# A decoder layer on one core: a third table of expert tiles, row scatters over more tiles, and another order at the end

## The reference

```python
x = _layernorm(x + _L0_attn_ref(x, ...))          # 16 heads of 16, over 1024 tokens
x = _layernorm(x + _L0_xattn_ref(x, ctx_1024, ...))  # one head, 77 context rows
x = _layernorm(x + _L0_ffn_ref(x, ...))           # 8 experts, 2 for each token
```

```python
gate = jax.nn.softmax(xf @ gate_w + gate_b)
topv, topi = jax.lax.top_k(gate, K)               # K = 2
topv = topv / topv.sum(-1, keepdims=True)
...
h = jax.nn.relu(xf @ w1e + b1e)                   # 256 -> 1024
y = h @ w2e + b2e                                 # 1024 -> 256
return (acc + y * ce[:, None], None)
```

## Time and profile before

| | us |
|---|---|
| median of 3 runs | 1412.01 |
| lowest and highest | 1411.73, 1417.89 |
| the profiled execution's own time | 1415.77 |
| span in its trace | 1413.8 |
| PE busy in the span | 1363.8 |
| DVE busy | 1063.5 |
| ACT busy | 858.8 |
| POOL busy | 592.2 |
| mean granted TensorE clock | 0.991 |

### The profile page before, as it was taken

One profiled execution on the slowest core, in us unless ns is written; L12 is line 12 of the kernel. 1 busy time (PEld: TensorE's weight loads), 2 busy tenths in 40 slices (PEclk: granted clock), 3 DMA queues, 4 the chain that ended last, 5 costly groups with the idle time before them and its releaser, 6 DMA issues.

```text
span 1413.8 us, 49461 instructions
## 1 busy us (share of the span) xinstructions
PE 1363.8 (96%) x18332; PEld 981.6 (69%) x18332; DVE 1063.5 (75%) x1989; ACT 858.8 (61%) x1903; POOL 592.2 (42%) x1058
## 2 busy tenths in 40 slices
PE   9999999999999999999999899989988999999995
PEld 5445454577777765456554458988877999999995
DVE  6888888888888888889999865756655566666564
ACT  4688888888887877778887784653222333333331
POOL 3221212222323224542223523566775556555555
PEclk9999999999999999999999999999999999999998
DMA  6236545544444323422423343333433333333332
GB/s 207 79 93 184 170 146 168 140 125 124 113 121 140 90 68 90 124 80 66 149 75 88 92 164 98 88 104 90 138 116 93 91 95 96 96 94 95 93 96 65
DMA packets 149816, 157.04 MB, mean 111 GB/s; under 512 B 68971, under 2 KB 121514, under 8 KB 148554
## 3 DMA queue, kind: packets, MB, share of 16 engines
q1 hardware_dynamic: 134922, 114.25, 29.8%
q0 software_dynamic: 14080, 38.32, 8.1%
q10 hardware_dynamic: 576, 1.31, 0.3%
HBM read 90.74 MB, written 63.04 MB: 109 GB/s over the span
## 4 chain that ended last, share of the span: by engine, by line
PE 77%; DVE 7%; issue 6%; POOL 5%; DMA 1%; ACT 1%; SPq 1%; another core or an unknown queue 1%; DVEq 1%; POOLq 0%; ACTq 0%
PE pa L1048 15%; PE pb L1048 14%; PE po L1220 14%; PE pa L1294 13%; PE pb L1308 11%; PE px L1048 8%; DVE neg L1582 3%; PE pb L1041 1%; POOL y_parts L995 1%; POOL out L989 1%; POOL x_by_expert L901 1%; PE px L1041 1%; DMA space<-y_parts,y_tags 1%; ACT w_sb L1414 1%
## 5 line engine op out<-in xcount | busy, mean ns | idle before, releaser
L1582 DVE TENSOR_REDUCE neg<-pa 128x1 f32<-128x1024 f32 x512 | 611.6, 1213 | 66.6 <-PE pa L1048 53.0
L1414 ACT ACTIVATE w_sb<-pb 128x512 f32<-128x512 f32 x996 | 589.2, 599 | 112.7 <-PE pb L1048 74.1
L1048 PE MATMUL pb<-w_sb 99*32 99x512 bf16 x3984 | 417.2, 381 | 5.8 <-ACT w_sb L1414 3.2
L1512 ACT ACTIVATE space<-pa,b1T_sb 128x128 f32<-128x128 f32 x568 | 154.6, 383 | 318.3 <-PE pa L1294 159.6
L1048 PE MATMUL pa<-w_sb 96*32 96x512 bf16 (+1 forms) x4208 | 335.3, 379 | 6.0 <-DVE neg L1582 5.5
L1220 PE MATMUL po<-w_sb,space 128*32 128x256 f32 x4000 | 315.6, 379 | 0.4 <-issue 0.3
L1294 PE MATMUL pa<-xgT,attn_t 128*128 128x128 f32 x2272 | 271.7, 278 | 14.8 <-DVE xgT L1869 11.8
L1294 PEld LDWEIGHTS pa<-xgT,attn_t 128*128 128x128 f32 x2272 | 268.1, 194 | 23.5 <-DVE xgT L1869 15.5
L1308 PE MATMUL pb<-w_sb,space 128*128 x1136 | 263.0, 382 | 0.4 <-issue 0.4
L1308 PEld LDWEIGHTS pb<-w_sb,space 128*128 128x128 f32 x1136 | 211.2, 192 | 27.0 <-issue 1.1
L1048 PEld LDWEIGHTS pa<-w_sb 96*32 96x32 bf16 (+1 forms) x4208 | 127.9, 97 | 109.3 <-DVE neg L1582 34.0
(11 more groups left out here) (251 smaller groups left out, 1230.7 us busy)
## 6 DMA issues: line engine op xcount, KB each, us to landing
y_parts<-attn_t SPq DMA_DIRECT2D x13, 896.0 KB, 4.9
xg<-x_by_expert SPq DMA_DIRECT2D x71, 130.0 KB
w_sb<-w SPq DMA_DIRECT2D x17, 512.0 KB, 4.6
attention_out<-space SPq DMA_DIRECT2D x64, 128.0 KB
w_sb<-w SPq DMA_DIRECT2D x7, 1024.0 KB
q_parts<-w_sb SPq DMA_DIRECT2D x48, 128.0 KB, 3.1
w_sb<-q_parts SPq DMA_DIRECT2D x64, 96.0 KB, 2.3
w_sb<-k_parts SPq DMA_DIRECT2D x64, 96.0 KB, 2.4
```

What stands on the lines that cost most here:

```text
L1048: mm = pe.matmul(out[at:end], lhsT[:, at:end], rhs, start=start, stop=stop, tile_position=(0, at))
L1414: act.activation(ex_of(n)[:, half * HALF:(half + 1) * HALF], score_bank(n, half), ACT.Exp, scale=SCALE).then_inc(e_done, 1)
L1512: ins = act.activation(hT[tile % 2][:, f, :], pH[tile % 2][:, f, :], ACT.Relu, bias=g.b1_sb[:, bass.ds(e * FT + f, 1)])
L1582: dve.tensor_reduce(neg[i % 2][:, t:t + 1], pa[n % 2][:, :], AX.X, ALU.max, negate=True).then_inc(max_done, 1)
```

## The change

It has five parts.

1. A table in the middle, `TABLE_M`, is made from batches 0 to 2 and covers tiles 25 to 40 (`MIDDLE` = 41). `later_tiles` replaces `late_tiles` and makes both later tables. The new one takes four stages, at the ends of token tiles 6 to 9 on VectorE, in rooms of their own (`hot`, `both`). The last table covers 30 tiles instead of 46.
2. SyncE's wait ahead of tile 25 asks for the middle table and batch 2's second rows; the wait for batch 3, the last table and the padding moves to tile 38, ahead of tile 41.
3. The row scatters go one to a tile from tile 7, two in tiles 12, 15, 18, 21, 24 and 27 (`TWO_ROWS` + 2), the last in tile 32.
4. GpSimd's order in the last two tiles: `scatter(69)` goes ahead of `scatter_out(68)`, and `gather(70)` ahead of `spread_3(69)`; `scatter_out(70)` counts on a semaphore of its own and no longer waits for `scatter_out(69)` to land.
5. VectorE reads the last tile's expert number from `table` at the start of tile 70 instead of just ahead of its `raw`.

```diff
-    EARLY = 3 * TB + 1
+    EARLY, MIDDLE = 3 * TB + 1, 5 * TB + 1
...
-    ROWS_AT = range(5, 21)
+    TWO_ROWS = (10, 13, 16, 19, 22, 25)
+
+    def rows_at(since):
+
+        first = sum(2 if n in TWO_ROWS else 1 for n in range(5, since))
+        return [row for row in range(first, first + (2 if since in TWO_ROWS else 1)) if since >= 5 and row < 4 * TB]
...
+        TABLE_M = TABLE_2 + ["left_1", "left_2", "left_3", "early"]
...
                         if tile + 3 == EARLY:
+                            sp.wait_ge(table_1, len(TABLE) + len(TABLE_M))
+                            sp.wait_ge(second_rows[B - 2], 16 * TB)
+                        if tile + 3 == MIDDLE:
                             sp.wait_ge(table_2, len(TABLE_2))
-                            for b in range(2, B):
-                                sp.wait_ge(second_rows[b], 16 * TB)
+                            sp.wait_ge(second_rows[B - 1], 16 * TB)
                             sp.wait_ge(pads_in, 16 * NE)
...
                     pool.wait_ge(c_normed, tile + 1)
-                    if tile:
+                    if 0 < tile < FFN_TILES - 1:
                         pool.wait_ge(out_rows, 16 * tile)
                     settle(pool, settled_pool)
                     pool.indirect_dma_start(g.out, bass.IndirectOffsetOnAxis(y_tag[tile % TAGS][:, 3:4], 0),
-                                            x3[tile % YS], None, bounds_check=Y_ROWS - 1).then_inc(out_rows, 16)
+                                            x3[tile % YS], None, bounds_check=Y_ROWS - 1
+                                            ).then_inc(out_rows if tile < FFN_TILES - 1 else last_out, 16)
...
-                    rows = [2 * (since - ROWS_AT[0]) + i for i in range(2)] if since in ROWS_AT else []
+                    rows = rows_at(since)
...
                     if LAST_TOKENS + 1 < tile < FFN_TILES - 1:
                         scatter_out(tile - 2)
+                    if tile == FFN_TILES - 1:
+                        scatter_out(tile - 2)
+                        gather(tile)
                     if tile:
                         spread_3(tile - 1)
...
-                    gather(tile)
+                    if tile < FFN_TILES - 1:
+                        gather(tile)
                     for row in rows[len(ahead):]:
                         scatter_row(row)
-                    if with_tokens(tile) or tile == FFN_TILES - 2:
+                    if with_tokens(tile):
...
+                def later_tiles(stage, first, last):
+                    n = last - first
+                    done, names = (len(TABLE), TABLE_M) if last < FFN_TILES else (0, TABLE_2)
+                    made = table_1 if last < FFN_TILES else table_2
+
+                    def after(name):
+                        dve.wait_ge(made, done + names.index(name) + 1)
...
+                        up_to = 0 if last < FFN_TILES else P - 1
+                        dve.tensor_scalar(full_i[:, :], g.run[:, :], float(up_to), None, ALU.add).then_inc(made, 1)
...
+                    if stage == 3:
+                        after("row_0")
+                        dve.tensor_tensor(left[:, :], tiles[:, :], cum[:, :], ALU.subtract).then_inc(made, 1)
+                        after("left_1")
+                        dve.tensor_scalar(left[:, :], left[:, :], float(n), 0.0, ALU.add, ALU.max).then_inc(made, 1)
+                        after("left_2")
+                        dve.tensor_tensor(left[:, :], left[:, :], tiles[:, :], ALU.min).then_inc(made, 1)
+                        after("left_3")
+                        dve.tensor_tensor(early[:, :], early[:, :], left[:, :], ALU.add).then_inc(made, 1)
...
-                def raw(tile):
-                    e = number(dve, tile, 1)
+                def raw(tile, e=None):
+                    e = number(dve, tile, 1) if e is None else e
...
+                    if SHIFT + 4 <= tile < SHIFT + 8:
+                        later_tiles(tile - SHIFT - 4, EARLY, MIDDLE)
...
-                    if since >= 4:
-                        late_tiles(since - 4)
+                    if 4 <= since < 7:
+                        later_tiles(since - 4, MIDDLE, FFN_TILES)
...
                 for tile in range(FFN_TILES):
+                    if tile == FFN_TILES - 1:
+                        last_e = number(dve, tile, 1)
...
-                result(FFN_TILES - 1)
+                result(FFN_TILES - 1, last_e)
```

More of the change, by code:

```diff
@@ L333, in stream @@
         top_f = sb("top_f", [P, TB, 2])
-        hot = [sb(f"hot{i}", [P, TB, NE]) for i in range(2)]
+        hot_room = sb("hot", [P, 2 * TB * NE])
+        hot = [hot_room[:, i * TB * NE:(i + 1) * TB * NE].rearrange("p (t e) -> p t e", e=NE) for i in range(2)]
         both = sb("both", [P, TB, NE])
@@ L1801, in early_tiles @@
                         dve.tensor_tensor(early[:, :], early[:, :], tiles[:, :], ALU.min).then_inc(table_1, 1)
-                def late_tiles(stage):
-                    n = FFN_TILES - EARLY
-                    slots = g.step_c[:, g.col["tiles"]][:, 0:n]
-                    past = late_room[:, 0:n * NE].rearrange("p (t e) -> p t e", e=NE)
-                    expert, before_e = (late_room[:, n * (NE + i):n * (NE + i + 1)] for i in range(2))
+                def later_tiles(stage, first, last):
[4 more added lines that the diff above has]
+                        dve.wait_ge(made, done + names.index(name) + 1)
+                    slots = g.step_c[:, g.col["tiles"]][:, 0:n]
+                    if last < FFN_TILES:
+                        past = hot_room[:, 0:n * NE].rearrange("p (t e) -> p t e", e=NE)
+                        expert, before_e = (both_room[:, n * i:n * (i + 1)] for i in range(2))
+                    else:
+                        past = late_room[:, 0:n * NE].rearrange("p (t e) -> p t e", e=NE)
+                        expert, before_e = (late_room[:, n * (NE + i):n * (NE + i + 1)] for i in range(2))
@@ L1814, in late_tiles @@
-                        dve.wait_ge(table_2, tabled_2("shift"))
-                        dve.tensor_copy(tiles[:, :], full_i[:, :]).then_inc(table_2, 1)
-                        dve.wait_ge(table_2, tabled_2("tiles"))
-                        dve.tensor_tensor(tiles[:, :], tiles[:, :], early[:, :], ALU.subtract).then_inc(table_2, 1)
-                        dve.wait_ge(table_2, tabled_2("late"))
-                        settle(dve, g.settled)
-                        dve.tensor_tensor_scan(cum[:, :], g.ones[:, 0:NE], tiles[:, :], 0.0, ALU.mult, ALU.add).then_inc(table_2, 1)
@@ new lines, in later_tiles @@
+                        after("shift")
+                        dve.tensor_copy(tiles[:, :], full_i[:, :]).then_inc(made, 1)
+                        after("tiles")
+                        dve.tensor_tensor(tiles[:, :], tiles[:, :], early[:, :], ALU.subtract).then_inc(made, 1)
+                        after("late")
+                        settle(dve, g.settled)
+                        dve.tensor_tensor_scan(cum[:, :], g.ones[:, 0:NE], tiles[:, :], 0.0, ALU.mult, ALU.add).then_inc(made, 1)
+                        dve.tensor_tensor(step[:, 0:NE - 1], early[:, 1:NE], early[:, 0:NE - 1], ALU.subtract).then_inc(made, 1)
@@ new lines, in later_tiles @@
+                        dve.tensor_scalar(step[:, NE - 1:NE], early[:, NE - 1:NE], -1.0, None, ALU.mult).then_inc(made, 1)
+                        after("step_last")
+                        dve.tensor_tensor(step[:, :], tiles[:, :], step[:, :], ALU.subtract).then_inc(made, 1)
+                    if stage == 1:
+                        dve.tensor_tensor(past, wide(slots, False, n), wide(cum[:, :], True, n), ALU.is_ge).then_inc(made, 1)
+                        after("past")
+                        dve.tensor_reduce(expert, past, AX.X, ALU.add).then_inc(made, 1)
+                        after("expert")
+                        dve.tensor_tensor(past, past, wide(step[:, :], True, n), ALU.mult).then_inc(made, 1)
+                        after("weighted")
+                        dve.tensor_reduce(before_e, past, AX.X, ALU.add).then_inc(made, 1)
@@ new lines, in later_tiles @@
+                    if stage == 2:
+                        after("before")
+                        dve.tensor_tensor(before_e, slots, before_e, ALU.subtract).then_inc(made, 1)
+                        after("row")
+                        dve.tensor_scalar(before_e, before_e, early[:, 0:1], None, ALU.add).then_inc(made, 1)
+                        after("row_0")
+                        dve.tensor_scalar(before_e, before_e, float(P), None, ALU.mult).then_inc(made, 1)
+                        after("rows_128")
+                        dve.scalar_tensor_tensor(g.table[:, 0, first:last], expert, float(ROWS_E), before_e, ALU.mult,
+                                                 ALU.add).then_inc(made, 1)
+                        dve.tensor_scalar(g.table[:, 1, first:last], expert, float(NE - 1), None, ALU.min).then_inc(made, 1)
@@ L1994, in raw, with result @@
```

(4 more changed lines are left out.)

39 lines of the change are left out of this document (11 added, 28 removed).

## The result

The changed kernel takes **1395.19 us** (median of 4 runs, 1393.45 to 1398.06); the kernel before, with one more run beside the three above, takes 1413.77. The ratio is 0.9867, with a 95% interval of 0.9837 to 0.9897: faster by 1.3%. I had forecast 1392.7 from 1412.01, a ratio of 0.9863. Its span is 17.7 us shorter than that of before; tiles 12 to 24 alone are 19.1 us shorter.

A forecast was written before the change was run, and what follows sets the result against it. TensorE was taken as the bound, losing 20.9 us in tiles 12 to 24, with GpSimd the engine to budget. Terms -20.9 + 3.7 + 1.0 - 5.3 + 2.7 - 0.5 = -19.3 us gave 1392.7 from median 1412.01; range 1386 to 1404.

The forecast's parts named there:

- The wait moves: SyncE's wait, tile 22 to 38: passed without stopping, removing 8.3 us of idle time and slow clock at tile 24.
- Row scatters over tiles 7 to 32, padding, last table: Tiles 12 to 32: the 12.6 us lost over tiles 12 to 23 replaced by losses of 3.7 and 1.0.
- The 1.0 for padding and last table: Tiles 13 to 16: VectorE's padding and last-table work still loses 1.0 us, bounds 0 and 3.
- The 3.7 for GpSimd: Tiles 12 to 32: GpSimd's 151.4 us of work exceeds 147.7, all 3.7 taken as loss; bounds 0 and 14.
- GpSimd's budget: Plain tiles: 5.31 us of own work plus 1.3 per row scatter, 6.61 with one and 7.91 with two.
- Token tiles: Tiles 7 to 10: one row scatter instead of two should remove 5.3 us; bounds 0 and 5.3.
- The middle table: Token tiles 6 to 9: 21 more small VectorE instructions, 4.5 us, lose 2.7 us; bounds 0 and 4.5.
- The path that I had named: Token tiles: table stages delay VectorE's norm, which TensorE's transpose needs, with 0.56 us of slack, some 0.15 of it signal.
- the rival that these tiles give nothing: Token tiles: ScalarE's lateness stays and hides the table's work, 1395.3 us; included in the forecast range's chance of 0.68.
- The tail: Last tiles: earlier result scatter 69 and gather(70) gain 0.5 us; bounds -0.5 and 1.5.
- The own semaphore gives nothing: Last write: no gain from its separate semaphore, since the idle time ahead already ends with VectorE.
- The rule on copies: Plain tiles: two VectorE copies each hold GpSimd up 0.5 us, 21 us over 21 tiles, giving 1413.7 us.

The follow-up runs named there:

- pairs: old_tail with row scatters two a tile again (tiles 7 to 22), keeping the moved wait and middle table; 1400.3 us, 0.9920 of before.
- old_tail: The changed kernel with the last two tiles' old GpSimd order, one semaphore and the late expert-number read; 1397.23 us, 0.9879 of before.
- rows_to_35: The changed kernel with three tiles that take two row scatters instead of six, the last row scatter in tile 35; 0.9856 of before.
- after_again: The changed kernel measured once more without any edit; 1399.36 us, 0.9904 of before.
- table_later: The changed kernel with the middle table's four stages one tile later, in tiles 7 to 10; 1397.28 us, 0.9888 of before.
- tail_out_first: The changed kernel with the out scatter of tile 68 ahead of result scatter 69 and the gather of tile 70 in GpSimd's last round; 0.9860 of before.
- before_plus: The kernel before with 20 unread VectorE additions where the middle table's stages stand, nothing else of the change; 0.9991 of before.

## Why the prediction was right

The number came out (a ratio of 0.9863 forecast, 0.9867 measured, 0.9904 in the repeat). The moved wait and the spread of the row scatters, the two large terms, are right in kind and near in size. The token tiles are wrong, and that the total is close in spite of it is in part luck.

- *The wait moves*: shown by pairs. It stops SyncE nowhere. I had put 8.3 us on it, the stall of tile 24 with its slow clock; in tiles 21 to 24 it is worth 8.7 or 10.0.
- *Row scatters over tiles 7 to 32, padding, last table*: from a loss of 12.6 I had left 4.7, a gain of 7.9. By pairs against old_tail, where the pace alone differs, the spread gains 4.9; between before and the changed kernel this term and the wait are 16.2 forecast and 16.3 measured together (the other traces of this spread give 13.4 to 16.9). The 1.0 for padding and last table measured nothing: tiles 13 to 16 took 7.02 or 7.03. The 3.7 for GpSimd measured 4.5, but behind the two `reweight`s and not all along, which a mean over 21 tiles can't tell. GpSimd's budget holds for its cadence (7.61 against 7.91, 6.18 to 6.67 against 6.61), and rows_to_35 lost 2.1 us in tiles 12 to 35 where it said about 2. Tiles 12 to 24 in 93.28 are as forecast (92 to 97). Tiles 25 to 32 in 58.97 (under 59) are so by a hair: after_again, old_tail, table_later and tail_out_first took 59.35 to 61.21.
- *Token tiles*: the step that failed is "One row scatter instead of two should remove the 5.3 us". It removed nothing: with the middle table in both, pairs takes 47.40 and old_tail 47.24. Tile 8, forecast at 9.8, took 10.24. What went is ScalarE's late signal, and before_plus shows that work on VectorE alone removes it. With pairs and the middle table these tiles gain 1.4, with the spread 1.5.
- *The middle table*: priced at 2.7 of loss. In table_later the first stage's tile gets 1.4 back, and 0.8 remains over the five tiles, so the stages do cost something in a dense token tile, about as the 1.1 for the first said. The path that I had named is not in the rows. In tiles 7 to 11 of the changed kernel no wait of TensorE ends with a norm of VectorE; the longest are for a copy of ScalarE in cross-attention (`PE pb L1057 <- ACT prT L1465: 1.9, 3, 0.7`: us in total, times, longest). The 0.15 that I took off for a signal is 0.03 to 0.12 in rows of the kernel before, from a producer's end to the start of the instruction that waits for it. The stages' cost can't be had apart from the lateness that they remove. The two token terms, 2.6 gained together, measured 1.5, so the rival that these tiles give nothing (1395.3) fits the time as well as my sum; its ScalarE lateness, which should have stayed, went.
- *The tail*: forecast 0.5 of gain, measured 0.2 of loss. Neither end of my account held the two things that decide there: a stall of 2.5 us in front of the moved scatter, and a last drain that is 1.45 us shorter (4.88 to 3.42). The stall came back in after_again and table_later. "The own semaphore gives nothing" holds as I argued: the idle time ahead of the last write still ends with VectorE (1.35 us, `DVE space L2068`). And SyncE's end, which the semaphore could move, lies ahead of the end of GpSimd's drain.
- *The rule on copies* (the Trainium skill, page "SBUF — State Buffer", section "Who interferes with whom") would have given 1413.7 by my estimate. The cadence of 6.18 to 6.67 with one row scatter has no room for it; some result scatters do take 1.22 to 1.33 in place of 0.99.

Open: why a signal of TensorE reaches ScalarE 2.6 and 1.8 us late in tiles 8 and 9 of the kernel before. GpSimd's indirect DMAs back to back are the nearest thing in time. That they are the cause was argued and not shown, and so was the thought that the stall in the tail is a piece of what the drain works off; only that it goes with an early drain is shown.

## What to carry to other kernels

Split a change by the stretch of the trace and by the edit before believing a term: here the sum was right within 2 us of the first measurement while one term of 5 us had another cause. An engine's budget (its work in a tile from its waits, plus each added DMA) forecast its cadence well, but not in which tiles the delay would show. And when an edit wins several us in the loop but none in the time, look behind the last useful write: the instruction that closes the kernel can be the longer one.

## What the runs showed of the hardware

The drain on GpSimd that ends the block is no constant. It took 3.42, 3.94, 4.68, 4.88 or 10.26 us at the same place. Without early drains it was the same within 10 ns in all kernels with one spread of the row scatters, and changing the tail's order changed nothing, so it goes with the place of the row scatters in the loop; by what rule is not shown. A drain ten tiles after another took 4.4 us, one 34 tiles after it 9.5, yet 3.42 and 4.88 came up after the whole loop without any.

Waits that the profile gives no cause for stand at the same instruction in every trace of one order: 3.92 us in the tail of the changed kernel, after_again and table_later, 2.11 in that of old_tail and tail_out_first. With rows in pairs that stall is missing in the tail, but all three such traces have one of 2.86 or 2.87 us while TensorE is in tile 61, where it costs nothing. In the kernel before:

```profile
1336.37 1.16 POOL L973 DMA_INDIRECT space<-y_parts,y_tags  x1 [2.86 <-issue]
```

With the rows spread to tile 35, no wait of that kind stands in the tail, and the last drain is the long one. That stall and drain are one thing is not shown.
